# One-core Perceiver block with a routed MLP: weight folds, loads and waits in another order

## Chip, core and metric

The kernel runs on 1 core of one Trainium2 chip. The time is device microseconds of one launch. Before the change it is 768.01 us, the median of 3 runs (766.83 to 769.06).

## What is computed

16 batches of 64 tokens of width 512 pass through three residual layers. The first attends over 1601 context rows for each batch, under a mask, and ends in a layer norm with gain and bias. The second is self-attention among a batch's 64 tokens, of one head. The third sends each token to 2 of 8 experts.

```
x = x + LN(softmax(mask(norm(x) @ ctx.T / sqrt(512))) @ ctx) * gamma + beta
q, k, v = norm(x) @ W_qkv.T            # one head, 64 tokens of a batch
x = x + (softmax(q @ k.T / sqrt(512)) @ v) @ W_out.T
s = norm(x) @ router_w.T               # top 2 of 8, softmax over the two
x = x + sum_e w_e * (gelu(norm(x) @ w1[e].T) @ w2[e].T)
```

All of it is float32. There are 1024 tokens, in 8 tiles of 128 (two batches each).

## The kernel before

**Folds.** Query and key weights appear only as a product, and value and output weights too. So the kernel turns the weights on TensorE (`turn_pieces` for query and key, L757; `turn_weights` for value, L765) and multiplies them (`fold`, L773, 32 products in the profile's count): "m" goes to `scores_w`, "vo" to `values_high` and `values_low`, a high and a low part. `raw_v` and `raw_out` are the raw weights; "vo" is read by the self-attention of each tile (`values`, L879 to L881).

**Rounds.** A loop over r = 1 to 7 mixes three tiles. For tile r it computes the context scores (`scores`, L805, three blocks of 512 context rows, then `rest_scores` for the last 65). For tile r - 1 it turns probabilities (`turn_prob`, L826) and sums context rows (`sums`, L846, in the order of `PV_ORDER`: the rest, then blocks 0, 1, 2). For tile r - 2 it does self-attention: `keys` (L861), `own_scores` (L871), `values`, `turn_own_probs` (L887, the transpose of the exponentials that ScalarE made), `weigh` (L893), then turns the normed row for the router. For tile r - 3 it routes. The order on each engine is written out by hand, and PSUM banks go round in the order of `fill_order()`.

**The other engines.** VectorE does the mask and the row maximum (`softmax`), the low part of a tile (`low_xn`, L1432), the gates and places of routing (`gates`, L1472 to L1477; `route_second`, L1483 to L1488), the layer norms (`queries`, L1350 to L1358, `second_norm`, `attended`, `first_norm`), and the maximum of the own scores (`tops`, L1421, with `copy_pt`, L1428). ScalarE does exponentials and copies. GpSimd turns a tile's mask into bounds (`bounds`, L619), adds the bias (L625), and writes and reads the routing table. SyncE issues nearly all loads: the turned context (L510) and the context (L497), 1024 KB for each batch and block, each when the buffer's former reader is done; the mask (L516) when the bounds of the tile before are ready.

**End of attention and experts.** After the loop tile 7 is finished, while the first expert's weights arrive. They come as float32 and are split: ScalarE writes the high part (`split_high`), VectorE the low part (`split_low`, L1501). The rows of the first expert are gathered on GpSimd (L672), and the tokens of tiles 6 and 7, which come too late for the gather, are added by one-hot products (`hot_rows`, L930), for which VectorE first casts a list of place numbers (L1562). `keep_busy` issues transposes whose result nobody reads. Then each expert runs 16 chunks: `up`, gelu, and `down` two chunks behind (`LAG`). For the last expert VectorE scales each token tile by its gate (L1669) and GpSimd adds it to the output by an indirect DMA (L707).

## Times and profile before

| what | us |
|---|---|
| median of 3 runs | 768.01 |
| profiled execution, its own time | 767.6 |
| its span | 765.9 |
| TensorE busy in the span | 736.6 (96%) |
| VectorE busy | 443.4 (58%) |
| ScalarE busy | 309.5 (40%) |
| GpSimd busy | 153.9 (20%) |
| moved by DMA | 199.40 MB |

The page divides the span into 40 slices of 19 us. Slices 1 to 17 are context attention, the next two its end and the routing, the rest the experts. In a timeline row stand the start, the duration, engine, line, operation, output and inputs, and in brackets how long the engine was idle before and what released it. Merged rows carry a count. A float32 product appears as two instructions in the profile's count (so L846 x20 is 10 in the program). Durations of merged TensorE rows overlap the next row by 0.07 us or so.

### The profile page before, as it was taken

Reading aid. Unit: us, or ns where it says so; the run is one execution under the profiler, and the core shown is the slowest. Engines: PE = TensorE matmul, PEld = TensorE weight load, DVE = VectorE, ACT = ScalarE, POOL = GpSimd, SP = SyncE. Lnnn points to the kernel's source line nnn. Section 1 sums busy time; section 2 is a strip of 40 time slices with the busy share of each in tenths; the row PEclk is TensorE's granted clock in tenths of the full one; section 3 lists DMA queues with packets and bytes.
Section 4 is the critical chain, followed back from the end, with each engine's and each line's share of the span. In section 5 each row is a group of like instructions: output and inputs, shape, how many; then the busy total and the mean of one; then the engine's idle time right before and its main releaser. Section 6 shows DMA issues by size and latency. Waiting matters only on the chain.

```text
span 765.9 us, 12386 instructions
## 1 busy us (share of the span) xinstructions
PE 736.6 (96%) x4794; PEld 560.5 (73%) x4794; DVE 443.4 (58%) x1005; ACT 309.5 (40%) x518; POOL 153.9 (20%) x162
## 2 busy tenths in 40 slices
PE   6999999999999999999999999999999999999992
PEld 5444455454545554578999999999998998888882
DVE  5243467676767664886775545555556556555620
ACT  2022212121223221335555555565555666666620
POOL 2132130404132200132310210310211230120201
PEclk9999999999999999999999999999999999999997
DMA  9999999999999999921545545655657565665302
GB/s 328 408 419 418 398 402 418 397 419 402 418 403 417 400 416 398 330 63 32 202 165 196 143 151 194 160 193 179 185 192 199 198 227 193 214 207 216 86 1 28
DMA packets 36333, 199.40 MB, mean 260 GB/s; under 512 B 4700, under 2 KB 5100, under 8 KB 15536
## 3 DMA queue, kind: packets, MB, share of 16 engines
q1 hardware_dynamic: 29912, 186.74, 63.2%
q0 software_dynamic: 4704, 9.14, 6.4%
q10 hardware_dynamic: 1656, 2.70, 1.0%
q8 instruction: 40, 0.66, 0.3%
q14 instruction: 21, 0.17, 0.1%
HBM read 188.19 MB, written 10.37 MB: 259 GB/s over the span
## 4 chain that ended last, share of the span: by engine, by line
PE 82%; DVE 11%; issue 2%; ACT 2%; DMA 1%; POOL 0%; DVEq 0%; POOLq 0%; ACTq 0%
PE ps L805 11%; PE ps L1066 8%; PE ps L1068 8%; PE ps L1067 8%; PE ps L846 7%; PE ps L1088 4%; PE ps L1089 4%; PE ps L1090 4%; PE ps L1095 4%; PE ps L1096 4%; PE ps L1097 4%; PE ps L773 4%; DVE xn_parts L1432 2%; PE ps L826 2%; PE ps L780 1%
## 5 line engine op out<-in xcount | busy, mean ns | idle before, releaser
L479 POOL TENSOR_TENSOR small<-small 128x1 f32<-128x1 f32 x64 | 24.1, 377 | 556.3 <-DVE yb_space L1669 197.4
L1068 PE MATMUL ps<-xT,low_a 128*128 128x288 f32 (+5 forms) x384 | 110.1, 287 | 0.0
L1274 ACT ACTIVATE hid<-ps 128x288 f32<-128x288 f32 (+5 forms) x128 | 50.6, 396 | 143.7 <-PE ps L1068 141.1
L1638 DVE TENSOR_TENSOR h_ring<-hid,h_ring 128x288 fp32r<-128x288 f32 (+5 forms) x128 | 55.7, 436 | 86.1 <-ACT h_ring L1279 86.0
L1501 DVE TENSOR_TENSOR low_a<-w_raw_a,high_b 128x2048 fp32r<-128x2048 f32 x32 | 73.4, 2292 | 39.2 <-ACT high_b L1202 39.2
L846 PE MATMUL ps<-arena 128*64 128x512 f32 (+1 forms) x416 | 94.1, 597 | 0.8 <-DVE arena L1401 0.8
L805 PE MATMUL ps<-arena 128*64 128x512 f32 x384 | 85.5, 596 | 0.2 <-ACT arena L1149 0.2
L1142 ACT COPY arena<-ps 128x512 f32<-128x512 f32 (+2 forms) x89 | 41.4, 525 | 100.6 <-PE ps L780 61.3
L1066 PE MATMUL ps<-xT,high_b 128*128 128x288 f32 (+5 forms) x256 | 74.9, 292 | 0.0
L1067 PE MATMUL ps<-xT,high_b 128*128 128x288 f32 (+5 forms) x256 | 73.4, 287 | 0.0
L1068 PEld LDWEIGHTS ps<-xT,low_a 128*128 128x128 f32 x384 | 72.4, 189 | 0.0
L846 PEld LDWEIGHTS ps<-arena 128*64 128x64 f32 (+1 forms) x416 | 27.9, 136 | 54.1 <-issue 51.8
L805 PEld LDWEIGHTS ps<-arena 128*64 128x64 f32 x384 | 26.3, 137 | 48.5 <-issue 47.8
L1202 ACT CAST high_b<-w_raw_a 128x2048 fp32r<-128x2048 f32 x32 | 60.8, 1904 | 0.0
L1090 PE MATMUL ps<-h_ring,low_a 128*128 128x288 f32 (+2 forms) x192 | 56.9, 296 | 0.0
L1279 ACT CAST h_ring<-hid 128x288 fp32r<-128x288 f32 (+5 forms) x128 | 53.4, 418 | 4.1
L1066 PEld LDWEIGHTS ps<-xT,high_b 128*128 128x128 f32 x256 | 48.3, 189 | 1.4
L1067 PEld LDWEIGHTS ps<-xT,high_b 128*128 128x128 f32 x256 | 48.3, 189 | 1.1
L1501 DVE TENSOR_TENSOR low_b<-w_raw_b,high_c 128x2048 fp32r<-128x2048 f32 x16 | 36.7, 2293 | 20.6 <-ACT high_c L1202 20.5
L1501 DVE TENSOR_TENSOR low_a<-w_raw_a,high_a 128x2048 fp32r<-128x2048 f32 x16 | 36.6, 2292 | 19.9 <-ACT high_a L1202 19.9
L619 POOL TENSOR_SCALAR arena<-arena 128x1601 f32<-128x1601 int32 x8 | 45.0, 5624 | 0.0
L1377 DVE SCALAR_TENSOR_TENSOR arena<-arena,ps 128x1024 f32<-128x1024 f32 (+1 forms) x16 | 15.3, 956 | 44.8 <-PE ps L805 44.8
(217 smaller groups left out, 1644.7 us busy)
## 6 DMA issues: line engine op xcount, KB each, us to landing
arena<-in_ctx_turned SPq DMA_DIRECT2D x48, 1024.0 KB, 20.4
arena<-in_ctx SPq DMA_DIRECT2D x48, 1024.0 KB, 18.7
w_raw_a<-in_w SPq DMA_DIRECT2D x48, 1024.0 KB, 4.8
w_raw_b<-in_w SPq DMA_DIRECT2D x16, 1024.0 KB, 4.8
arena<-in_mask SPq DMA_DIRECT2D x8, 800.5 KB, 22.1
tokens_x<-arena SPq DMA_DIRECT2D x11, 256.0 KB, 12.4
arena<-in_w_qkv SPq DMA_DIRECT2D x8, 256.0 KB, 4.8
out<-res SPq DMA_DIRECT2D x8, 256.0 KB, 9.2
```

Source lines behind the costliest of these rows:

```text
L619: pool.tensor_scalar(bound, mask_sb, 0, MASKED - LIMIT, ALU.is_equal, ALU.mult).then_inc(bound_ready, 1)
L805: mm = pe.matmul(bank(blk)[64 * b:64 * b + 64, :], xqT[:, k, 64 * b:64 * b + 64], ctxT[blk][:, b, k, :], start=(k == 0), stop=(k == KC - 1))
L846: mm = pe.matmul(att_ps[64 * b:64 * b + 64, :], probT[0:m, c, 64 * b:64 * b + 64], rows, start=(n == 0 and c == chunks[0]), stop=(n == NBL ...
L1066: pe.matmul(o, w_high[2 * f][:, cols], high[:, k, 0:w.width], start=(k == 0), stop=False)
L1067: pe.matmul(o, w_high[2 * f][:, cols], low[:, k, 0:w.width], start=False, stop=False)
L1068: mm = pe.matmul(o, w_low[2 * f][:, cols], high[:, k, 0:w.width], start=False, stop=(k == KC - 1))
L1090: mm = pe.matmul(o, low[:, cols], h_high[:, 0:w.width], start=False, stop=final)
L1202: act.copy(w_high[j], w_raw[j]).then_inc(w_high_ready, 1)
L1274: nc.scalar.activation(hid[:, c % 2, 0:w.width], bank(c % UP_BANKS)[:, 0:w.width], ACT.Gelu).then_inc(gelu_done, 1)
L1279: act.copy(h_ring[:, c % RING, 0, 0:w.width], hid[:, c % 2, 0:w.width]).then_inc(h_high_ready, 1)
L1501: dve.tensor_tensor(w_low[j], w_raw[j], w_high[j].bitcast(F32), ALU.subtract).then_inc(w_ready, 1)
L1638: dve.tensor_tensor(h_ring[:, c % RING, 1, 0:w.width], hid[:, c % 2, 0:w.width], h_ring[:, c % RING, 0, 0:w.width].bitcast(F32), ALU.subtr ...
```

## The change

- Loads: value and output weights are loaded first, in eight pieces, then tile 0, then query and key weights; the constants come in two DMAs, the identity by itself first.
- Folds: value weights are turned piece by piece, and the fold "vo" comes first. Query and key weights are turned behind it, and the fold "m" comes behind tile 0's scores and the turning of tile 1's query. `bank_at`, `by_act` and the order of copies follow.
- A round: blocks 0 and 1 of `sums` move behind `turn_own_probs` and `weigh`; VectorE's `tops` moves ahead of `queries`.
- End of attention: the low part of the first expert's block 1 is made on GpSimd; `low_xn(LAST - 1)` moves ahead of `attended(LAST)`; two `keep_busy` grow or are added.
- Last expert: behind its last `up`, chunks 13, 14 and 15 of `down` are done for token tile 0 and then for token tile 1.

TensorE at the start of the program, before (L757 and L765 are transposes of weights, L773 a fold, L805 scores of tile 0, L826 the turned probabilities):

```order
L938 MATMUL ps<-cst 128x128 x16
L757 MATMUL ps<-cst,arena 128x128 x32
L773 MATMUL ps<-arena 128x512 x16
L780 MATMUL ps<-cst,arena 128x128 x4
L792 MATMUL ps<-cst,arena 128x65 x8
L805 MATMUL ps<-arena 64x512 x24
L815 MATMUL ps<-arena 64x65 x8
L765 MATMUL ps<-cst,arena 128x128 x16
L773 MATMUL ps<-arena 128x512 x16
L780 MATMUL ps<-cst,arena 128x128 x4
L792 MATMUL ps<-cst,arena 128x65 x8
L826 MATMUL ps<-cst,arena 65x128
```

and after (L760 transposes, L775 a fold, L807 scores, L828 probabilities):

```order
L940 MATMUL ps<-cst 128x128 x6
L760 MATMUL ps<-cst,arena 128x128 x16
L775 MATMUL ps<-arena 128x512 x16
L760 MATMUL ps<-cst,arena 128x128 x32
L782 MATMUL ps<-cst,arena 128x128 x4
L794 MATMUL ps<-cst,arena 128x65 x8
L807 MATMUL ps<-arena 64x512 x24
L817 MATMUL ps<-arena 64x65 x8
L782 MATMUL ps<-cst,arena 128x128 x4
L794 MATMUL ps<-cst,arena 128x65 x8
L775 MATMUL ps<-arena 128x512 x16
L828 MATMUL ps<-cst,arena 65x128
```

One fold and 16 transposes moved ahead of the scores, the other fold behind them.

VectorE in one round, before, from the queries (L1350 to L1358), which follow the places, to the tops (L1421):

```order
L1350 BN_STATS small<-res 128x6
L474 MEMSET small 128x1
L1352 BN_AGGR small<-small 128x2
L1334 TENSOR_SCALAR small<-small 128x1
L1335 TENSOR_SCALAR small<-small 128x1
L1336 SCALAR_TENSOR_TENSOR small<-small 128x1
L1338 SCALAR_TENSOR_TENSOR small<-small 128x1
L1340 SCALAR_TENSOR_TENSOR small<-small 128x1
L1342 SCALAR_TENSOR_TENSOR small<-small 128x1
L1344 SCALAR_TENSOR_TENSOR small<-small 128x1
L1358 TENSOR_SCALAR arena<-res,small 128x512
L1421 TENSOR_REDUCE small<-ps 64x1 x2
```

and after, from the places (L1488) on:

```order
L1488 TENSOR_TENSOR route<-ps,route 128x8
L1490 TENSOR_TENSOR route<-route 128x16
L1492 TENSOR_REDUCE route<-route 128x2
L1493 CAST route<-route 128x2
L1426 TENSOR_REDUCE small<-ps 64x1 x2
L1427 TENSOR_SCALAR small<-small 128x1
L473 MEMSET small 128x1
L1355 BN_STATS small<-res 128x6
```

The tops (L1426) are now the first thing behind the places, and the queries (L1355) follow.

GpSimd at the end of attention, before, from the last gathers (L672) to the sends of routing rows (L642):

```order
L672 DMA rows_space<-tokens_x,route 128x512
L479 TENSOR_TENSOR small<-small 128x1
L672 DMA rows_space<-tokens_x,route 32x512
L630 TENSOR_TENSOR small<-small 128x1
L479 TENSOR_TENSOR small<-small 128x1
L642 DMA slots_m<-route 9216x16 x2
```

and after, from the last gathers (L671) to the sends of routing rows (L641):

```order
L671 DMA rows_space<-tokens_x,route 128x512
L478 TENSOR_TENSOR small<-small 128x1
L671 DMA rows_space<-tokens_x,route 32x512
L478 TENSOR_TENSOR small<-small 128x1
L698 TENSOR_TENSOR low_a<-w_raw_a,high_a 128x2048
L629 TENSOR_TENSOR small<-small 128x1
L478 TENSOR_TENSOR small<-small 128x1
L641 DMA slots_m<-route 9216x16 x2
```

The split (L698) is new; it stands between the gather and the sends.

The diff, cut to its core:

```diff
@@ -70,16 +70,15 @@
 def fill_order():
-    for which in ("wq", "wk", "m"):
+    for which in ("wv", "vo", "wq", "wk"):
         for n in range(KC):
...
         yield kind, 0, 0
-    for which in ("wv", "vo"):
-        for n in range(KC):
-            yield which, 0, n
     for kind in ("xq", "rest0", "rest1"):
         yield kind, 1, 0
+    for n in range(KC):
+        yield "m", 0, n
     for r in range(1, TILES):
...
@@ -524,16 +523,16 @@
...
                 sp.dma_start(tokens_x[t * P:(t + 1) * P, :], xr[t % 2]).then_inc(x_out[t % 2], 16)
-            for raw, first, here in ((raw_q, 0, wq_in), (raw_k, KC, wk_in)):
+            for raw, of, first, here in ((raw_v, w_qkv, 2 * KC, wv_in), (raw_out, w_out, 0, wo_in), (raw_q, w_qkv, 0, wq_in),
+                                         (raw_k, w_qkv, KC, wk_in)):
                 for k in range(KC):
-                    sp.dma_start(raw[:, k, :], w_qkv[:, (first + k) * D:(first + k + 1) * D]).then_inc(here[k], 16)
-            sp.dma_start(res[:, 0:D], x[0:P, :]).then_inc(x_in, 16)
+                    sp.dma_start(raw[:, k, :], of[:, (first + k) * D:(first + k + 1) * D]).then_inc(here[k], 16)
+                if raw is raw_out:
+                    sp.dma_start(res[:, 0:D], x[0:P, :]).then_inc(x_in, 16)
             load_rest(0)
...
                 load_turned(0, blk)
-            sp.dma_start(raw_v, w_qkv[:, 2 * WBLK:].rearrange("p (k h) -> p k h", k=KC)).then_inc(wv_in, 16)
-            sp.dma_start(raw_out, w_out.rearrange("p (k h) -> p k h", k=KC)).then_inc(wo_in, 16)
             load_rest(1)
...
@@ -543,7 +542,7 @@
...
             load_mask(2)
-            sp.wait_ge(filled, filled_at("vo", 0, KC - 1))
+            sp.wait_ge(filled, filled_at("m", 0, KC - 1))
             load_ctx(0, 1)
...
@@ -693,6 +692,10 @@
...
             gather(STATIC[0], 3)
+            pool.wait_ge(w_high_ready, 2)
+            pool.wait_ge(w_ready, 1)
+            carry_pool_waits(pool, own)
+            pool.tensor_tensor(w_low[1], w_raw[1], w_high[1].bitcast(F32), ALU.subtract).then_inc(w_ready, 1)
             for t in range(LAST - 1, TILES):
...
@@ -759,17 +762,16 @@
...
                             mm.then_inc(filled, 1)
-            def turn_weights(kind, raw, hc):
-                o = open_fill(kind, 0, hc)
-                for k in range(KC):
-                    mm = pe.transpose(o[:, k * P:(k + 1) * P], raw[:, k, hc * P:(hc + 1) * P], ident)
-                mm.then_inc(filled, 1)
-
             def fold(kind, left, right):
...
                     for hc in range(KC):
+                        if kind == "vo" and m == 0:
+                            wait_copied(pe, "wv", 0, hc)
+                            pe.wait_ge(wo_in[hc], 16)
+                        if kind == "m" and m == 0:
+                            wait_copied(pe, "wk", 0, hc)
                         mm = pe.matmul(o, left[:, hc, m * P:(m + 1) * P], right[:, hc, :],
...
@@ -937,26 +939,23 @@
...
                     pe.transpose(o[:, 0:P], ident, ident)
-            pe.wait_ge(cst_in, 16)
-            keep_busy(16, bank(0))
+            pe.wait_ge(id_in, 16)
+            keep_busy(6, bank(0))
+            turn_pieces("wv", raw_v, wv_in)
+            fold("vo", turned_v, raw_out)
             turn_pieces("wq", raw_q, wq_in)
+            wait_copied(pe, "vo", 0, KC - 1)
             turn_pieces("wk", raw_k, wk_in)
-            for n in range(KC - 2, KC):
-                wait_copied(pe, "wk", 0, n)
-            fold("m", turned_q, turned_k)
             turn_query(0)
             turn_rest(0)
+            wait_copied(pe, "wq", 0, KC - 1)
             for blk in range(NBLK - 1):
...
             rest_scores(0)
-            pe.wait_ge(wv_in, 16)
-            for hc in range(KC):
-                turn_weights("wv", raw_v, hc)
-            pe.wait_ge(wo_in, 16)
-            wait_copied(pe, "wv", 0, KC - 1)
-            fold("vo", turned_v, raw_out)
             turn_query(1)
             turn_rest(1)
+            fold("m", turned_q, turned_k)
+            pe.wait_ge(cst_in, 16)
             for r in range(1, TILES):
...
@@ -977,14 +976,14 @@
...
                 sums(r - 1, PV_ORDER[0])
-                sums(r - 1, PV_ORDER[1])
                 if runs(r - 2):
...
                     turn_own_probs(r - 2)
-                sums(r - 1, PV_ORDER[2])
+                sums(r - 1, PV_ORDER[1])
                 if runs(r - 2):
                     weigh(r - 2)
+                sums(r - 1, PV_ORDER[2])
                 sums(r - 1, PV_ORDER[3])
...
@@ -1019,8 +1018,10 @@
...
             router(LAST)
-            keep_busy(18, open_fill("rank", LAST))
+            keep_busy(23, open_fill("rank", LAST))
             ranks(LAST)
+            wait_copied(pe, "logit", LAST)
+            keep_busy(5, bank(bank_at("logit", LAST)))
             hot_rows(LAST)
...
@@ -1091,20 +1092,27 @@
...
                     for t, (a, m) in enumerate(w.tiles):
+                        if only is not None and t != only:
+                            continue
                         o = bank(y_bank(w, t))[0:m, :]
...
                             mm.then_inc(first_tile_done, 1)
-                mm.then_inc(down_done, 1)
+                if only != 0:
+                    mm.then_inc(down_done, 1)
             for w in STATIC:
...
                     up(w, c)
-                    if c >= LAG:
+                    if w.kind == EXPERTS - 1 and c == FC - 1:
+                        for t in range(2):
+                            for late in range(FC - 1 - LAG, FC):
+                                down(w, late, t)
+                    elif c >= LAG:
                         down(w, c - LAG)
...
@@ -1117,9 +1125,6 @@
...
                     more = in_use(pe)
-            for c in range(FC - LAG, FC):
-                down(STATIC[-1], c)
-
             with pe.If(more > 0):
...
@@ -1201,28 +1206,28 @@
...
                 act.copy(w_high[j], w_raw[j]).then_inc(w_high_ready, 1)
-            act.dma_start(cst[:], consts).then_inc(cst_in, 16)
-            act.wait_ge(cst_in, 16)
-            act.copy(small[:, 26:27], me)
-            for kind, dst in (("wq", turned_q), ("wk", turned_k)):
-                for n in range(0, KC, 2):
-                    copy_fill(kind, 0, dst[:, n, :], n)
+            act.dma_start(ident, consts[:, C_ID:C_ID + P]).then_inc(id_in, 16)
+            act.wait_ge(id_in, 16)
+            act.copy(small[:, 26:27], ident[:, 0:1])
+            for n in range(0, KC, 2):
+                copy_fill("wv", 0, turned_v[:, n, :], n)
+            act.dma_start(cst[:, C_TRI:], consts[:, C_TRI:]).then_inc(cst_in, 16)
             act.dma_start(res[:, D:2 * D], x[P:2 * P, :]).then_inc(x1_in, 16)
...
             act.dma_start(rw_sb, w_router.rearrange("p (k e) -> p k e", k=KC)).then_inc(rw_in, 16)
-            for n in range(0, KC, 2):
-                copy_fill("m", 0, scores_w[:, n, :], n)
-            copy_query(0)
-            copy_rest(0)
-            for n in range(KC):
-                copy_fill("wv", 0, turned_v[:, n, :], n)
-            exps(0)
             for n in range(KC):
...
                 act.copy(values_high[:, n, :], bank(bank_at("vo", 0, n))).then_inc(vo_high, 1)
-            copy_query(1)
-            copy_rest(1)
+            for kind, dst in (("wq", turned_q), ("wk", turned_k)):
+                for n in range(0, KC, 2):
+                    copy_fill(kind, 0, dst[:, n, :], n)
+            for p in range(2):
+                copy_query(p)
+                copy_rest(p)
+            exps(0)
+            for n in range(0, KC, 2):
+                copy_fill("m", 0, scores_w[:, n, :], n)
             act.wait_ge(zero_out, 16)
...
@@ -1509,23 +1514,25 @@
...
             own.then_next(dve.memset(cum[0], 0.0))
+            for n in range(1, KC, 2):
+                copy_fill("wv", n, turned_v[:, n, :])
+            queries(0)
             dve.wait_ge(cst_in, 16)
...
                 own.then_next(dve.memset(capacity[:, p:p + 1], float(WIDTHS[p])))
-            for kind, dst in (("wq", turned_q), ("wk", turned_k)):
-                for n in range(1, KC, 2):
-                    copy_fill(kind, n, dst[:, n, :])
-            queries(0)
-            for n in range(1, KC, 2):
-                copy_fill("m", n, scores_w[:, n, :])
-            softmax(0)
-            queries(1)
             for n in range(KC):
...
                                   ).then_inc(copied[False], 1)
+            for kind, dst in (("wq", turned_q), ("wk", turned_k)):
+                for n in range(1, KC, 2):
+                    copy_fill(kind, n, dst[:, n, :])
+            queries(1)
+            softmax(0)
+            for n in range(1, KC, 2):
+                copy_fill("m", n, scores_w[:, n, :])
             for r in range(1, TILES):
...
@@ -1535,22 +1542,22 @@
...
                     route_second(r - 3)
+                if runs(r - 2):
+                    tops(r - 2)
                 if runs(r + 1):
...
                 if runs(r - 2):
-                    tops(r - 2)
                     copy_pt(r - 2)
...
             route_first(LAST - 2)
-            for j in range(2):
-                split_low(STATIC[0], j)
+            split_low(STATIC[0], 0)
             gates(LAST - 2)
             route_second(LAST - 2)
+            low_xn(LAST - 1)
             attended(LAST)
-            low_xn(LAST - 1)
             tops(LAST - 1)
...
@@ -1567,6 +1574,7 @@
...
             second_norm(LAST)
+            dve.wait_ge(w_ready, 2)
             split_low(STATIC[0], 2)
```

## Rows read from the trace of the kernel before

**Rows 1.** The page's slices: busy DMA in tenths, and GB/s.
```profile
DMA  9999999999999999921545545655657565665302
GB/s 328 408 419 418 398 402 418 397 419 402 418 403 417 400 416 398 330 63 32 202 165 196 143 151 194 160 193 179 185 192 199 198 227 193 214 207 216 86 1 28
```

**Rows 2.** Timeline of TensorE, tile 0's scores and the fold behind them.
```profile
29.41 10.52 PE L805 MATMUL ps<-arena 128*64 128x512 f32 x48 [0.19 <-ACT arena L1149]
...
43.17 13.97 PE L773 MATMUL ps<-arena 128*128 128x512 f32 x32 [0.88 <-issue]
```

**Rows 3.** SyncE's loads: tile 0's last turned blocks (L510), tile 4's mask (L516).
```profile
L510 SPq DMA_DIRECT2D arena<-in_ctx_turned x2: 522/523/524, 8.8 to 9.4; - x2
...
DMA to landing us min/median/max: 20.3/21.6/22.8
...
L516 SPq DMA_DIRECT2D arena<-in_mask x1: 327/327/327, 107.2 to 107.2; - x1
...
DMA to landing us min/median/max: 27.8/27.8/27.8
```

**Rows 4.** Timeline of TensorE in rounds 3 (146.78) and 4.
```profile
146.78 0.33 PE L887 MATMUL ps<-cst,own_space 128*128 128x128 f32 x1 [1.48 <-ACT own_space L1183]
...
175.18 4.51 PE L846 MATMUL ps<-arena 65*64 65x512 f32 x20
...
183.24 0.33 PE L887 MATMUL ps<-cst,own_space 128*128 128x128 f32 x1
```

**Rows 5.** Timeline of GpSimd and VectorE in rounds 3 and 4.
```profile
135.28 5.61 POOL L619 TENSOR_SCALAR arena<-arena 128x1601 f32<-128x1601 int32 x1
...
142.32 0.69 DVE L1350 BATCH_NORM_STATS2 small<-res 128x6 f32<-128x512 f32 x1
...
178.78 0.69 DVE L1350 BATCH_NORM_STATS2 small<-res 128x6 f32<-128x512 f32 x1
...
181.68 0.47 DVE L1421 TENSOR_REDUCE small<-ps 64x1 f32<-64x64 f32 x2
```

**Rows 6.** Two lines of VectorE over the span: ns least/median/most.
```profile
L1432 DVE TENSOR_TENSOR xn_parts<-arena,xn_parts x8: 682/1810/4309, 99.5 to 332.7; 128x512 fp32r<-128x512 f32 x8
...
L1472 DVE CAST route<-route x8: 158/606/1052, 139.9 to 351.8; 128x2 int32<-128x2 f32 x8
```

**Rows 7.** TensorE's waits: us in total, times, longest.
```profile
PE ps L879 <- DVE xn_parts L1432: 0.7, 1, 0.7
```

**Rows 8.** Timeline of VectorE at the end of attention.
```profile
312.34 4.49 DVE L1501 TENSOR_TENSOR low_a<-w_raw_a,high_a 128x2048 fp32r<-128x2048 f32 x2 [1.05 <-ACT high_a L1202]
...
333.29 0.30 DVE L1562 CAST arena<-arena 128x288 f32<-128x288 int32 x1
...
334.47 0.48 DVE L1421 TENSOR_REDUCE small<-ps 64x1 f32<-64x64 f32 x2 [0.87 <-PE ps L871]
...
338.45 0.29 DVE L1428 COPY own_space<-ps 128x128 f32<-128x128 f32 x1 [0.32 <-PE ps L887]
```

**Rows 9.** Timeline of GpSimd: the bias of one tile, the last gather.
```profile
255.10 1.28 POOL L625 TENSOR_TENSOR res<-res,arena 128x512 f32<-128x512 f32 x1
...
332.97 1.17 POOL L672 DMA_INDIRECT rows_space<-tokens_x,route  x1
```

**Rows 10.** Hot rows of tiles 6 and 7; one microsecond with its granted clock (0.50).
```profile
342.77 2.21 PE L930 MATMUL ps<-arena 128*128 128x288 f32 x8
...
351.25 3.66 PE L930 MATMUL ps<-arena 128*128 128x288 f32 x8 [0.66 <-DVE arena L1496]
...
352.00:353.00 1.00, 1.00 (x4) 0.70 (x3) 0.90 (x5) 0.40 (x1) 0.19 (x1) 0.50 0.00 0
```

**Rows 11.** Chain of waits at the end: start, us, what.
```profile
751.33 0.24 PE ps L1097
...
751.60 0.76 DVE yb_space L1669
...
755.19 1.48 POOL out L707
```

12 lines of the change are left out of this document (6 added, 6 removed).

## Prediction

> **What bounds the kernel now.** I read the engine totals first: TensorE is busy 96% of the span, so time can only come from its waits, from work done at a low clock, and from the two ends. The list of waits names few: the start, a transpose that waits for a ScalarE exponential (L887), products that wait for the low part of a tile (L879) [rows 7]. The page's slices of DMA show a second resource at its limit: about 410 GB/s without a pause until some 325 us, that is, through the whole attention stage [rows 1]. TensorE never waits for DMA there, but it is not far ahead of it. So every microsecond saved at the front has to be checked against landings, and every order inside a round against VectorE. All times below are from one profiled execution of 767.6 us (span 765.9), 0.4 under the median of the runs, 768.0. I work out a difference and add it to the median.
>
> **Part 1, the opening.** Value and output weights (8 pieces of 256 KB, 2.1 MB) now go ahead of query, key and tile 0's context; the fold of value and output comes first and the fold of query and key behind tile 0's scores. TensorE's work is the same but for 10 fewer filler transposes. What changes is the landing of tile 0's turned context. Its last block was issued at 9.4 us and landed 22.8 later, at 32.2 [rows 3], and scores began at 29.41 with three blocks in 10.52 us, so the third block was read at 36.4 [rows 2], 4 us behind its landing. With 2.1 MB more ahead of it in the queue, at 0.41 MB/us [rows 1], it lands at 37.3. However early TensorE gets to the scores, they end at 37.3 + 3.5 = 40.8 rather than 39.9. The gain comes behind them: before, 3.2 us lay between the end of the scores (39.93) and the start of the second fold (43.17) [rows 2], mostly transposes of the value weights and a short wait; these now lie ahead of the scores, where the landing hides them. With the scores 0.9 later, I put the front at some 2 us earlier from round 1 on (3.2 less 0.9, a little more or less for the copies behind the fold).
>
> The waits that the opening adds hold nothing up that I can find. Key's transposes wait until VectorE has split the last value fold, while query's 16 transposes run. SyncE's wait ahead of context blocks 1 and 2 is now for the fold of query and key, which ends where the other one ended. VectorE's wait for the constants, now a separate DMA, stands behind the first queries and ahead of the value splits; TensorE needs those only for the keys, some 10 us on. If the constants landed that late, the loss would still lie under the wait for the context.
>
> I count none of it. Round 3 is tied to something that does not move: the mask for tile 4. It was issued at 107.2, when the bounds of tile 3 were ready, and landed 27.8 us later, at 135.0 [rows 3], behind a queue whose bytes are the same after the change. At 135.28 GpSimd starts on it for 5.61 us, until 140.9 [rows 5]. VectorE's operations that need the port which GpSimd then holds stand still: L1432, at best 682 ns, took 4309 in this round, and the small cast L1472, 158 ns at best, 1052 [rows 6]. The chain to tile 1's exponentials goes through that cast, so TensorE's L887 of round 3 has a floor in absolute time.
>
> **Part 2, the order inside a round.** TensorE's sums of the first large block go behind own scores, values and the transpose L887; VectorE looks for the own tops (L1421) ahead of the next tile's queries. Two things follow. The tops can start where the queries started: 142.32 in round 3, 178.78 in round 4 [rows 5]. From tops to the transpose it takes 183.24 - 181.68 = 1.56 us [rows 4, 5]. But one block of sums, 16 of the 20 instructions that took 4.51 us, 3.6 us [rows 4], now comes after the transpose rather than before it.
> - Round 3: L887 at 142.32 + 1.56 = 143.88, and with the block behind it 147.48, where the round before was at 146.78 (it had waited 1.48) [rows 4]. That is 0.70 later, whatever the opening had gained.
> - Round 4: 178.78 + 1.56 + 3.6 = 183.94 against 183.24: 0.70 more. TensorE itself would be ready for the transpose by about 183.24 - 3.6 = 179.6, against 180.34 from VectorE: a new wait of 0.7. Rounds 5 and 6 repeat round 4's rows (three of this kind in all), so 0.70 each.
> - Round 2 has no gating work for VectorE and round 7 no bounds on GpSimd; I count 0 there. In round 2 the transposed probabilities (L1428) now stand behind queries that GpSimd blocks, up to a microsecond, but round 3 swallows that.
> Sum for the rounds: 4 x 0.70 = 2.8 us later. The bounds are 0 (if VectorE is released sooner) and, with the front's gain kept as well, -2; on the other side +5, should L1428, which now stands behind the queries (2.9 us from 178.78 to 181.68), hold `weigh` up by half a microsecond more in each.
>
> **Part 3, the end of attention.** One of VectorE's two splits of expert weights (4.49 us for two, 2.25 each [rows 8]) goes to GpSimd, and the low part of tile 6 is ahead of the long `attended(LAST)`. The wait of 0.7 us at L879 goes [rows 7], and I shift VectorE's work behind it by 0.7. But GpSimd's split has a place and a price. GpSimd does it behind the gather, whose last part started at 332.97 and took 1.17 [rows 9]. The gather hangs on the routing that stood behind the two splits, so it ends 2.25 earlier, at 331.9, and the split starts near 332.1. A GpSimd tensor_tensor of 128x512 takes 1.28 us [rows 9]; four times that is 5.1. Below it is VectorE's 2.25 for the same tensor, above nothing nearer. In this time, from 332.1 to 337.4, VectorE wants the cast of place numbers (L1562), at 333.29 - 0.7 = 332.6 [rows 8]. It has the short form of L1472's kind (288 columns in 0.30 us), so I take it to be blocked as L1472 was. Tops of tile 7 then start near 337.7 rather than at 334.47: 3.2 later. Of that 0.32 comes back where VectorE had waited at L1428 [rows 8]. Cost 2.9 us, since from there VectorE and TensorE alternate until the experts begin. The bounds are -0.7 (no blocking) and +5.1 (all of it in the way). VectorE's new wait for that split, ahead of its third one, is met long before; so are GpSimd's sends behind it, whose gates come after VectorE's routing.
>
> The Trainium skill (GPSIMD Engine Reference, section on elementwise cost) gives 4.5 us on GpSimd for a tensor_tensor of 2048 float32 columns against 2.29 on VectorE. The second agrees with the trace here; by the first the cost of this part would be 2.3 rather than 2.9.
> The trace shows the blocking only beside L619, a GpSimd operation of one input. The Trainium skill (SBUF — State Buffer, "Who interferes with whom") states that it holds against any GpSimd operation that reads SBUF, for VectorE operations of two SBUF inputs or in a two-port mode, and that the one that issues first keeps the port. By it the routing operations behind the cast would be held back even if the cast got through, and the cost would be about 1 us.
>
> **Part 4, filler and clock.** Before, the hot rows of tile 7 took 3.66 us where the same eight instructions for tile 6 took 2.21, with the granted clock at 0.50 in that stretch, the 1.2 GHz level, after some 2 us in which TensorE did little [rows 10]. Five more filler transposes ahead of the ranks and five behind them close that gap and fit into the waits that they fill. Gain 1.45, if the clock holds; 0 if not; a loss of 1.2 if all ten delay the ranks (128 columns each where one of the eight, 0.28 us, had 288: 0.12).
>
> **Part 5, the last expert.** Behind the last `up`, TensorE did three chunks for both token tiles, tile 0's last product being followed by tile 1's. VectorE scaled tile 0 at 751.60 and GpSimd sent out the second part at 755.19, two sends in a row [rows 11]. Now all of tile 0 comes first: its result is ready 6 products earlier, of 0.24 us each [rows 11], 1.4 us, less some 0.2 for the last hidden chunk, which now has less cover. GpSimd's sends are serial, so both go out 1.2 earlier; tile 1's own result comes at most 0.2 later and finds the queue free. Gain 1.2, at least 0.5, at most 1.4.
>
> **Sum.** +2.8 + 2.9 - 1.45 - 1.2 = +3.05. On the profiled execution this is 770.6, on the median 771.1. I forecast 770.8.
>
> **Rivals.**
> - A, the forecast: the rounds get a wait, GpSimd's split holds VectorE up, filler and end pay. 770.8, own range 769 to 772.5. For it: VectorE is the last releaser at L887 in both rounds that I read, and a port conflict is in the trace. Against it: starts of GpSimd's work are rough.
> - B, the split on GpSimd is free: it starts later than I think or doesn't hold the port. Part 3 is then -0.7 and the sum +2.8 - 0.7 - 1.45 - 1.2 = -0.55: 767.4, no change. This is the case that isn't slower. It decides at L1562: if the cast starts under 333.3, less what the rounds added, B holds. For it: the cast and GpSimd's start are within 0.5 us of each other in my working.
> - C, round 3 isn't pinned, VectorE finishes its routing before GpSimd takes the port, and the front's 2 us stay while rounds 4 to 6 lose nothing: -2 - 0.7 - 1.45 - 1.2 = -5.4: 762.6; with part 3's cost, 766.2. It needs VectorE to be more than 2.2 us earlier in round 3 than before; DMA allows about 1 there.
> - D, the clock falls as well: in A TensorE has, by my working, little to do for some 4 us ahead of the row products, longer than the 2 us that preceded the fall at 352. The row products (about 5 us) would then run at 1.65 times their length as the hot rows did, up to 3.3 more: 774.
>
> **Chances.** A 0.42, B 0.25, C 0.17, D 0.16. A measurement of this kernel can tell 0.3%, 2.3 us, from no change: faster is under 765.7, slower over 770.3. A gives 0.27 slower and 0.15 the same; D 0.16 slower; B 0.20 the same and 0.05 faster; C 0.04 the same and 0.13 faster. So faster 0.18, same 0.39, slower 0.43. The range 764.5 to 774 leaves out the better half of C and the far end of D.
>
> **What would show it.** In the changed profile: the third block of tile 0's scores waits for a landing near 37 us; L887's successor waits for ScalarE 3 us in round 3 and 0.7 in rounds 4 to 6, and the starts of rounds 4 to 7 stand 0.7, 1.4, 2.1 and 2.8 later than before; a VectorE cast of 128x288 takes 4 to 5 us beside GpSimd's split; the last hot rows take 2.2 us at a granted clock of 1.0; VectorE's two last scalings stand apart in start, by more than the 0.7 of one, rather than in one piece. The forecast is wrong if rounds 3 to 6 show no new wait at the transpose (C), or the cast takes 0.3 us (B).

## The result, and the profile after

The changed kernel takes 778.57 us (median, 775.22 to 780.16), the kernel before 767.42 in the same comparison: ratio 1.0137, 95% interval 1.0099 to 1.0176. It is slower by 1.4%, where 0.4% was forecast. The profiled execution took 778.62 us with a span of 777.0, so 11.1 more than the span of before. The page's slices, to be held against [rows 1]:

```profile
PEclk9999999999999999979999999999999999999997
DMA  8999999999999998910445644745665756574402
GB/s 299 385 417 418 395 402 417 400 419 401 419 401 417 398 416 353 338 60 29 147 163 179 171 148 167 212 127 216 170 226 173 211 185 229 188 244 171 126 1 27
```

Two things are new. The first two slices moved 299 and 385 GB/s, and one slice, from 330 to 350 us, has a granted clock of 0.7. The opening, on TensorE (start, duration, idle before and what ended it), to be held against [rows 2]:

```profile
29.28 3.65 PE L807 MATMUL ps<-arena 128*64 128x512 f32 x16 [0.27 <-ACT arena L1154]
35.73 3.65 PE L807 MATMUL ps<-arena 128*64 128x512 f32 x16 [2.80 <-DMA arena<-in_ctx_turned]
41.34 3.65 PE L807 MATMUL ps<-arena 128*64 128x512 f32 x16 [1.95 <-DMA arena<-in_ctx_turned]
46.38 1.93 PE L775 MATMUL ps<-arena 128*128 128x512 f32 x4
```

TensorE was ready for tile 0's scores when it was before, waited twice for landings, and read the third block at 41.3 rather than at the forecast 37.3. Windows of before and of after show most of the reason (length, busy time of each engine, granted clock, DMA share, GB/s):

```profile
5.00:10.00 5.00, 5.00 (x24) 5.00 (x25) 0.80 (x10) 0.13 (x1) 0.00 (x0) 1.00 1.04 373
10.00:20.00 10.00, 8.79 (x40) 5.47 (x39) 8.04 (x16) 2.74 (x5) 5.39 (x2) 1.00 1.03 387
20.00:30.00 10.00, 9.81 (x36) 4.79 (x36) 2.10 (x3) 1.73 (x4) 1.84 (x3) 1.00 1.03 415
```
```profile
5.00:10.00 5.00, 4.92 (x23) 4.55 (x22) 0.81 (x2) 1.07 (x2) 0.00 (x0) 1.00 0.92 289
10.00:20.00 10.00, 10.00 (x24) 4.30 (x24) 5.20 (x25) 1.17 (x2) 0.00 (x0) 1.00 1.06 359
20.00:30.00 10.00, 9.29 (x58) 6.41 (x58) 5.16 (x13) 4.46 (x9) 5.77 (x2) 1.00 1.02 392
```

From 5 to 30 us before moved 5 x 0.373 + 10 x 0.387 + 10 x 0.415 = 9.9 MB, after 9.0. The missing 0.9 MB are 2.3 us of the queue at 0.41 MB/us.

TensorE's waits from 121 to 300 us (us in total, times, longest), first of before, then of after:

```profile
PE ps L887 <- ACT own_space L1183: 1.6, 2, 1.5
```
```profile
PE ps L889 <- ACT own_space L1188: 3.3, 4, 1.5
```

The transpose of own probabilities waits 1.49 us in round 3 (1.48 before, [rows 4]) and 0.62, 0.60 and 0.60 in rounds 4 to 6. The wait of [rows 7], for the low part of a tile, is gone. Rounds 3 to 7 begin 2.97, 2.97, 3.47, 3.93 and 4.43 us later than before. The end of attention is where most is lost. VectorE, GpSimd and TensorE there:

```profile
336.58 4.64 DVE L1341 SCALAR_TENSOR_TENSOR small<-small 128x1 f32<-128x1 f32 x1
336.65 4.54 POOL L698 TENSOR_TENSOR low_a<-w_raw_a,high_a 128x2048 fp32r<-128x2048 f32 x1
342.10 0.55 DVE L1363 TENSOR_SCALAR arena<-res,small 128x512 f32<-128x512 f32 x1
342.70 1.11 PE L782 MATMUL ps<-cst,arena 128*128 128x128 f32 x4 [4.51 <-DVE arena L1363]
```

GpSimd's split took 4.54 us. A VectorE operation on one column, 0.22 us when nothing is in its way, took 4.64 beside it and ended at 341.22, 0.03 us behind the split. It belongs to tile 6's normalization, for which TensorE then waited 4.51 us. Behind that wait TensorE's clock was low (windows of TensorE: busy time, granted clock, DMA share, GB/s):

```profile
338.00:342.00 4.00, 0.19 (x2) 0.93 0.00 0
342.00:346.00 4.00, 3.30 (x26) 0.50 0.35 131
346.00:350.00 4.00, 4.00 (x12) 0.50 0.00 0
352.00:356.00 4.00, 3.73 (x28) 1.00 0.00 0
```

0.50 is the 1.2 GHz level. The products of tile 7's values started 0.43 us apart there, those of tile 6's values 0.23 us apart. The last hot rows, for their part, now ran at the full clock, to be held against [rows 10], and the two outputs of the last expert stood apart, to be held against [rows 11]:

```profile
364.93 2.21 PE L932 MATMUL ps<-arena 128*128 128x288 f32 x8
```
```profile
762.66 0.75 DVE L1677 TENSOR_SCALAR yb_space<-ps,route 128x512 f32<-128x512 f32 x1 [1.06 <-PE ps L1100]
764.75 0.75 DVE L1677 TENSOR_SCALAR yb_space<-ps,route 112x512 f32<-112x512 f32 x1 [1.34 <-PE ps L1100]
```

The 11.1 us between the two profiled executions divide as follows. Opening and rounds make 4.4 until round 7 begins. The sums of tile 7 behind the loop make 1.5; the granted clock fell to 0.50 there, between 310 and 315 us. From there to the transpose of tile 7's own probabilities it is 7.8 (351.77 against 338.08, 13.7 in all). Then the filler gains 1.5 and the last expert 1.1.

### The profile page after: what moved, and what is told of

Read it like the earlier page. It is cut to its first block, busy times and chain, and to the rows that moved or that the text cites. A ratio compares the mean times of both kernels' runs of the same rounds, so it can differ in the third digit from the quotient of the medians.

```text
span 777.0 us, 12399 instructions
## 1 busy us (share of the span) xinstructions
PE 741.4 (95%) x4794; PEld 562.3 (72%) x4794; DVE 440.4 (57%) x1006; ACT 308.6 (40%) x516; POOL 159.2 (20%) x164
## 4 chain that ended last, share of the span: by engine, by line
PE 79%; DVE 7%; DMA 6%; SPq 3%; issue 1%; ACT 1%; POOL 0%; DVEq 0%; POOLq 0%; ACTq 0%
PE ps L848 10%; PE ps L807 9%; PE ps L1067 8%; PE ps L1069 8%; PE ps L1068 8%; PE ps L1089 4%; PE ps L1090 4%; PE ps L1091 4%; PE ps L1098 4%; PE ps L1099 4%; PE ps L1100 4%; DMA arena<-in_ctx_turned 3%; DMA arena<-in_ctx 3%; PE ps L775 2%; PE ps L782 1%
## 5 line engine op out<-in xcount | busy, mean ns | idle before, releaser
L848 PE MATMUL ps<-arena 128*64 128x512 f32 (+1 forms) x416 | 96.0, 606 | 1.3 <-DVE arena L1406 0.9
L807 PE MATMUL ps<-arena 128*64 128x512 f32 x384 | 85.9, 596 | 5.4 <-DMA arena<-in_ctx_turned 5.2
L807 PEld LDWEIGHTS ps<-arena 128*64 128x64 f32 x384 | 26.4, 137 | 54.2 <-issue 46.4
L1506 DVE TENSOR_TENSOR low_a<-w_raw_a,high_a 128x2048 fp32r<-128x2048 f32 x15 | 34.4, 2292 | 19.9 <-ACT high_a L1207 19.9
```

Source lines behind the costliest of these rows:

```text
L807: mm = pe.matmul(bank(blk)[64 * b:64 * b + 64, :], xqT[:, k, 64 * b:64 * b + 64], ctxT[blk][:, b, k, :], start=(k == 0), stop=(k == KC - 1))
L848: mm = pe.matmul(att_ps[64 * b:64 * b + 64, :], probT[0:m, c, 64 * b:64 * b + 64], rows, start=(n == 0 and c == chunks[0]), stop=(n == NBL ...
L1506: dve.tensor_tensor(w_low[j], w_raw[j], w_high[j].bitcast(F32), ALU.subtract).then_inc(w_ready, 1)
```

## The experiments

Each was timed against the kernel before on the same chip. Ratios are to the kernel before, with 95% intervals. The experiments fall into three such comparisons, in which the kernel before took 767.69 us (1, 2, 4 and 6), 767.98 (3, 8, 9 and 10) and 768.22 (5, 7, 11 and 12). A gain or loss is counted from the one of its own comparison; between kernels of two comparisons, or against the changed kernel, some 0.5 us are uncertain from this alone.

**1. The change without GpSimd's split** (a_no_gpsimd_split).

```diff
...
-            pool.tensor_tensor(w_low[1], w_raw[1], w_high[1].bitcast(F32), ALU.subtract).then_inc(w_ready, 1)
...
-            split_low(STATIC[0], 0)
+            for j in range(2):
+                split_low(STATIC[0], j)
...
-            dve.wait_ge(w_ready, 2)
```

> The changed kernel, with one edit taken back: VectorE makes both low halves of expert weights behind round 7 (blocks 0 and 1), as before the change; GpSimd none. Theory S (GpSimd's 4.54 us split held VectorE's normalization of tile 6 for 4.64 us, and the low clock from 342 to 351 us followed from TensorE's 4.5 us wait): both go, at the price of 2.25 us of VectorE: about 4.5 + 3.8 - 0.5 = 7 to 9 us less than the changed kernel's 778.6, so 770 to 771. The transpose of attended rows that waited 4.51 waits under 2, and values of tile 7 run at 0.23 us per product. Rival R (the low clock at 342 is not the wait's doing, but comes by itself, as that at 309 to 316 did): only the 4 to 5 us of blocking go, 774, and a stretch at a granted clock of 0.50 remains between 335 and 360. Rival F (the split is free, the loss lies in the front and the rounds): within 1 us of 778.6.

Measured: 770.13 us (768.37 to 772.49), ratio 1.0031 (1.0012 to 1.0051). This one edit is worth 8.4 of the 11 us by the medians (8.1 by the ratios); the changed kernel has only four runs. TensorE in the same windows as above:

```profile
338.00:342.00 4.00, 4.00 (x27) 1.00 0.28 106
342.00:346.00 4.00, 3.77 (x28) 1.00 0.00 0
346.00:350.00 4.00, 3.71 (x23) 1.00 0.30 96
```

Both the wait and the low clock are gone, as theory S has it.

**2. The split alone** (b_split_only): on the kernel before, the reverse of the edit above.

> The kernel before, with one edit: the low half of expert weight block 1 is made by GpSimd behind its gather for tile 7, and VectorE makes one half fewer there. Theory S: GpSimd holds VectorE for 4 to 4.6 us at an operation that stands at about 326 to 332 us, TensorE waits 4 us or more behind it and the clock falls to 0.50 afterwards: +5 to +9, so 773 to 776. Theory A of the forecast (the cast of 288 columns is held, no fall of the clock): +2.9, 770.9. Rival F (free): -0.7 to 0, 767.3.

Measured: 772.28 us, ratio 1.0055 (1.0023 to 1.0087), and the widest spread of all: 767.49 to 778.37 in 12 runs. Four runs took 776.9 to 778.4 us at a mean granted clock of 0.982 to 0.984, three some 772.5 at 0.986, and five 767.5 to 771.1 at 0.990 to 0.993. So the long runs fit theory S and the shortest fit rival F. Only one run has a trace, 777.46 us, one of the long ones:

```profile
332.49 5.09 DVE L1342 SCALAR_TENSOR_TENSOR small<-small 128x1 f32<-128x1 f32 x1
```
```profile
333.04 4.51 POOL L699 TENSOR_TENSOR low_a<-w_raw_a,high_a 128x2048 fp32r<-128x2048 f32 x1
```

What is held is the small operation behind the one of the changed kernel, in the same normalization. Its row ends with the split (337.58 and 337.55) but starts 0.55 us ahead of it, while the last gather ran. The split's 4.5 us are fixed. That VectorE stands still for all of them or not at all, by what it has to do as the split starts, is how I read the spread; no short run of this kernel has a trace that would show it.

**3. Filler in TensorE's wait** (a_filler_wait).

```diff
+            keep_busy(36, open_fill("xr", LAST - 1))
             turn_second(LAST - 1)
```

> The changed kernel, with 36 more filler transposes (some 0.12 us each, 4.3 us) ahead of the transposes of tile 6's normalized rows, where TensorE waits 4.5 us for VectorE, which GpSimd's split holds. The split stays on GpSimd. Theory S (the fall to a granted clock of 0.50 from 342 to 351 us follows from TensorE's wait): the clock stays at 1.00, values of tile 7 take 0.23 us per product, and the time is 3 to 4 less than 778.6, 774.6 to 775.6; the wait for VectorE stays. Rival R (the fall has another cause, the long attention stage): a stretch of 0.50 of some 9 us remains and the time is 778.6.

Measured: 775.09 us (771.98 to 776.68), ratio 1.009 (1.0072 to 1.0107), 3.5 under the changed kernel. The mean granted clock of its six runs is 0.987 to 0.995, that of the changed kernel's four 0.983 to 0.990. Time and clock are those of theory S, but the profile doesn't prove it: in the profiled run, the fastest of the six, GpSimd's split started behind all of tile 6's normalization and held nothing that TensorE waited for.

```profile
336.99 0.37 DVE L1570 CAST arena<-arena 128x288 f32<-128x288 int32 x1
```
```profile
337.40 4.54 POOL L698 TENSOR_TENSOR low_a<-w_raw_a,high_a 128x2048 fp32r<-128x2048 f32 x1
```

There the filler itself was in the way (TensorE was in it from 336.27 to 340.2) and the clock stayed at 1.00. That the clock falls behind a wait and stays up without one is seen in five traces at the end of attention: it fell to 0.50 in experiments 2 and 4 and in the changed kernel, behind waits of 4.5 us and more, and in experiment 5 behind one of 1.86, and did not fall in experiment 1. That filler alone holds it up through a held normalization stays open.

**4. Query and key weights in one transfer each** (a_qk_whole).

```diff
+                if raw is raw_q or raw is raw_k:
+                    sp.dma_start(raw, of[:, first * D:(first + KC) * D].rearrange("p (k h) -> p k h", k=KC)).then_inc(here[0], 16)
+                    continue
```

> The changed kernel, with query weights and key weights each loaded by one transfer of 1 MB, whose rows are 8 KB, in place of four of 256 KB with rows of 2 KB. Theory L (small rows lower the rate of the first 20 us, 268 to 390 GB/s where the kernel before had 373 to 420): the rate from 6 to 24 us rises to about 400, the third block of tile 0's turned context lands at 38 to 39 rather than 41.3, and the time falls by 1 to 2.5 us, 776 to 777.5. Rival H (the rate is that of the hardware's start, whatever the rows): landing unchanged within 0.5 us; the transposes of the query weights start later, as their four pieces come together, and the time is the same or up to 2 us more.

Measured: 777.55 us (776.32 to 778.48), ratio 1.0115 (1.0084 to 1.0146). The third block of tile 0 was read at 38.91 instead of 41.34, and scores of tile 1 began at 59.38 instead of 61.82, 2.4 us sooner, so theory L is right for the landing. Of that 1.5 us were gone again when round 3 began, at 123.55 against 124.45. The time is 1 us under the changed kernel's, which is within both intervals. Two of the waits of its round 2:

```profile
88.97 3.65 PE L810 MATMUL ps<-arena 128*64 128x512 f32 x16 [0.86 <-DMA arena<-in_ctx_turned]
94.07 3.65 PE L810 MATMUL ps<-arena 128*64 128x512 f32 x16 [0.86 <-DMA arena<-in_ctx_turned]
```

TensorE had caught up with the transfers there. What the opening gains beyond them is lost again. GpSimd's split held VectorE in this kernel too: the same operation as in the changed kernel took 4.95 us and ended with the split, at 340.65.

```profile
335.70 4.95 DVE L1344 SCALAR_TENSOR_TENSOR small<-small 128x1 f32<-128x1 f32 x1
```
```profile
336.10 4.52 POOL L701 TENSOR_TENSOR low_a<-w_raw_a,high_a 128x2048 fp32r<-128x2048 f32 x1
```

**5. GpSimd's split behind tile 6's normalization** (a_split_late).

```diff
             pool.wait_ge(w_ready, 1)
+            pool.wait_ge(xn_split, TILES)
```

> The changed kernel, with one more wait: GpSimd begins its split only when VectorE has written the low part of tile 7, that is behind tile 6's normalization. Theory S (the 4.6 us hold falls on whatever VectorE issues as the split starts; what matters is that it was the normalization, for which TensorE waits): VectorE's normalization takes its 0.22 us, TensorE's wait there falls from 4.5 to about 1 us, the clock stays at 1.00: 769.5 to 772. Rival T (VectorE's later operations of two inputs, tops and routing of tile 6, are held in turn until the split ends): the hold moves, 773 to 776, and the spread over runs gets smaller than that of the changed kernel.

Measured: 773.58 us (772.5 to 774.38), ratio 1.0072 (1.005 to 1.0093), and the narrowest spread of the kernels with a split (1.9 us; experiment 4, whose split isn't tied, has 2.2). Rival T is right. GpSimd's split, and VectorE beside it:

```profile
339.52 4.58 POOL L699 TENSOR_TENSOR low_a<-w_raw_a,high_a 128x2048 fp32r<-128x2048 f32 x1
```
```profile
339.06 0.30 DVE L1570 CAST arena<-arena 128x288 f32<-128x288 int32 x1
340.49 0.48 DVE L1427 TENSOR_REDUCE small<-ps 64x1 f32<-64x64 f32 x2 [1.12 <-PE ps L874]
341.00 0.15 DVE L1428 TENSOR_SCALAR small<-small 128x1 f32<-128x1 f32 x1
341.60 0.16 DVE L1459 TENSOR_REDUCE route<-route 128x1 f32<-128x8 f32 x1
341.79 2.33 DVE L1462 SCALAR_TENSOR_TENSOR route<-route,cst 128x8 f32<-128x8 f32 x1
344.16 0.16 DVE L1464 TENSOR_REDUCE route<-route 128x1 f32<-128x8 f32 x1
```

Reductions and a one-column operation on one input and constants go through at their usual length. The first operation with two inputs from SBUF stands until the split ends at 344.10. TensorE then waited 1.86 us for routing, and the clock was at 0.50 from 348 to 350. This kernel is 5.4 us over the kernel before and experiment 1 is 2.4 over it, so the split, moved out of the worst place, still costs 3 us.

**6. The new opening alone** (b_front_only): weight loads, folds and copies as in the change, all else as before.

> The kernel before, with the new opening alone: value and output weights in 8 pieces ahead of query and key, their fold first, the fold of query and key behind tile 0's scores, identity and constants as two transfers. Order inside the rounds, filler, last expert and splits as before. Theory L (landings set the opening: 5 us of the queue's early rate is lost to the 8 more transfers of 2 KB rows): third block of tile 0's context lands at 41, scores of tile 1 1 to 1.5 us later, and the rounds, tied to the masks' landings, +1.5 to +3: 769.5 to 771. Forecast's own step: 0 (the front gains 2, round 3 takes it back): 768. Rival G (the fronts' loss is absorbed by the wait of 1.48 us at round 3's transpose): within 0.5 us of before.

Measured: 769.38 us (767.05 to 772.97), ratio 1.0022 (1.0003 to 1.0042), 1.7 slower. The third block of tile 0 was read at 40.46, scores of tile 1 began 0.6 later than before and round 3 2.0 later. The wait in round 3 shrank from 1.48 to 0.52, so that rounds 4 to 7 began 1.07 later. Theory L and rival G share it: the landings come later, and the wait absorbs a part.

**7. The new opening with the output weights in one transfer** (b_front_out_whole): on experiment 6, one load of 1 MB for `raw_out`, and one wait for it.

> The kernel before with the new opening alone, and the output weights loaded by one transfer of 1 MB in place of four of 256 KB. Theory L1 (the dip to 170 to 270 GB/s between 5 and 8 us comes from the output weights' small rows): it goes, 10 us of queue deliver 2.8 MB as in the kernel before, not 2.3, third block of tile 0's context lands some 1 us sooner. Rival L2 (the dip has to do with the transfers of value weights and constants, or with two tensors at once): it stays, and the time is that of the opening alone, 769.4.

Measured: 767.59 us (765.09 to 769.76), ratio 1.0001 (0.9982 to 1.002). The dip between 5 and 10 us is mostly gone:

```profile
5.00:10.00 5.00, 3.92 (x21) 3.49 (x19) 1.19 (x2) 1.07 (x2) 0.00 (x0) 1.00 0.97 350
```

Scores of tile 1 began at 59.31, 1.6 sooner than in experiment 6. In the profiled runs with the old opening they began between 59.49 and 60.65 (six traces), in those with the new one and its loads in pieces between 60.94 and 62.81 (five), and with some of these loads whole between 59.18 and 59.38 (experiments 4, 7 and 12). So theory L1 holds for the landing, though TensorE itself came to tile 0's scores later here, at 31.96 rather than 29.34. The two intervals of the ratio overlap (1.0003 to 1.0042 in experiment 6), so a gain in time isn't shown.

**8. The order in the rounds alone** (b_rounds_only).

```diff
                 sums(r - 1, PV_ORDER[0])
-                sums(r - 1, PV_ORDER[1])
...
                     turn_own_probs(r - 2)
-                sums(r - 1, PV_ORDER[2])
+                sums(r - 1, PV_ORDER[1])
                 if runs(r - 2):
                     weigh(r - 2)
+                sums(r - 1, PV_ORDER[2])
                 sums(r - 1, PV_ORDER[3])
```

together with the edit of experiment 9.

> The kernel before, with the new order in the rounds alone: the second large block of sums goes behind own scores, values and the transpose of own probabilities, and VectorE looks for the own tops ahead of the next tile's queries. Theory W (each of rounds 4 to 6 waits 0.6 us at that transpose and takes 36.97 us instead of 36.5; round 3 waits 1.5, as before): +1.4 to +2.8, 769.1 to 770.5. Rival N (those waits come from the opening's delay, and with the old opening the rounds are free): within 0.5 of before.

Measured: 770.2 us (767.39 to 773.3), ratio 1.0026 (1.0012 to 1.004), 2.2 slower. Its waits are those of the changed kernel: 1.48 in round 3, 0.62, 0.62 and 0.61 in rounds 4 to 6, each of these rounds 36.97 us long against 36.46 to 36.52 before. Theory W holds. The transpose of round 4:

```profile
180.30 0.33 PE L887 MATMUL ps<-cst,own_space 128*128 128x128 f32 x1 [0.62 <-ACT own_space L1183]
```

**9. Tops ahead of the next queries, alone** (b_tops_only).

```diff
+                if runs(r - 2):
+                    tops(r - 2)
                 if runs(r + 1):
                     queries(r + 1)
                 if runs(r - 2):
-                    tops(r - 2)
                     copy_pt(r - 2)
```

> The kernel before, with one edit: VectorE looks for the own tops (some 1.5 us) ahead of the next tile's queries. The sums' order stays. Theory W: own probabilities are ready sooner by the queries' length, the waits at the transpose (1.48 in round 3, 0.16 in round 5) go, while the queries and what hangs on them have cover: -0.5 to -1.6, 766.1 to 767.2. Rival M (round 3 is tied to the mask's landing and GpSimd's bounds, the tops cannot start before): 0, 767.7.

Measured: 765.57 us (762.65 to 766.45), ratio 0.9963 (0.9946 to 0.9981), 2.4 faster, more than theory W allowed. No wait at the transpose is left, and rounds 3 to 6 take 36.13 us each. That goes for round 3 too, although GpSimd's bounds start at 136.19 in it, so rival M is refuted. The transpose of round 4, then VectorE in that round, first of experiment 9, then of experiment 8:

```profile
181.13 0.27 PE L887 MATMUL ps<-cst,own_space 128*128 128x128 f32 x1
```

```profile
178.69 0.48 DVE L1421 TENSOR_REDUCE small<-ps 64x1 f32<-64x64 f32 x2 [1.41 <-PE ps L871]
```
```profile
178.74 0.47 DVE L1421 TENSOR_REDUCE small<-ps 64x1 f32<-64x64 f32 x2
```

Counted from the round's start on TensorE (157.47 and 159.29), VectorE was ready for the tops after 19.8 us in experiment 9 (it then waited 1.41 for its input) and after 19.5 in experiment 8. Its chain is as long in both. But TensorE comes to the transpose after 23.7 us in experiment 9 and after 20.4 in experiment 8, where the probabilities are there after 21.0.

**10. Filler, last expert and the low part of tile 6, alone** (b_ends_only): the changed kernel's three edits of that kind on the kernel before.

> The kernel before, with the end of attention's filler (23 transposes ahead of the last ranks, 5 behind), the low part of tile 6 ahead of the attended rows of tile 7, and the last expert's order (all of token tile 0 first). No split on GpSimd, old opening and rounds. By the changed kernel's trace: filler -1.5 (hot rows 2.21 us at the full clock, not 3.66), last expert -1.1, low part -0.7 to 0: 764.5 to 765.2. Rival P (filler only moves the low clock elsewhere, or the last send is bound by the queue): 766.5 to 767.7.

Measured: 765.16 us (763.32 to 769.24), ratio 0.9962 (0.9948 to 0.9976), 2.8 faster, as the trace of the changed kernel had it. (Its profiled run, 769.24 us, is the slowest of the ten.)

**11. What gained, together** (c_tops_ends): experiments 9 and 10 on the kernel before.

> The kernel before, with the parts that gained when each was made alone: VectorE's tops ahead of the next queries (2.4 us less), and filler, last expert's order and early low part of tile 6 (2.8 us less). They lie in different stages, so they should add: 767.8 - 5.2 = 762.6. Rival Q (both gains partly hide one another, as with a wait for the masks or the clock's chance): 764 to 765.

Measured: 762.95 us (761.91 to 763.9), ratio 0.9938 (0.9917 to 0.9959). The two gains add: 2.4 + 2.8 = 5.2 expected, 5.3 measured. This kernel is faster than the changed kernel and than the kernel before.

**12. The same with the new opening, its loads whole** (c_tops_ends_front): only the value weights still come in four pieces.

> The same, with the new opening too, where output, query and key weights are loaded by one transfer of 1 MB each and only the value weights in four pieces. Theory L (the opening loses because the queue delivers 0.9 MB less in the first 30 us; with whole transfers most of that comes back): within 1 us of the kernel without the new opening, 762 to 763.5. Rival K (the new opening costs its 1.7 us through something else, such as the later issue of context blocks 1 and 2): 764.3 or more. Rival J (scores of tile 1 begin 1 us sooner than in the kernel before, and with the tops early nothing in round 3 takes it back): 761.5.

Measured: 762.57 us (761.87 to 764.02), ratio 0.9935 (0.9915 to 0.9956). With whole transfers the opening costs nothing, and gains nothing that these runs can tell. Scores of tile 1 began at 59.18 here and 60.65 in experiment 11, round 3 at 121.89 and 121.43, the transpose of round 7 came at 290.09 and 289.82. The 1.5 us are lost by round 3.

## Why the prediction was wrong, point by point

**Sign and size.** Slower was right and the likeliest case, but the time lay 4.6 us above the range. The largest error is in part 3: GpSimd's split, put at 2.9 us, cost 8.4.

**Part 1, the opening: the DMA term was mis-sized.** The forecast took 0.41 MB/us from the queue with 2.1 MB more in it. The third block was read as it landed, at 41.3, not 37.3. In the first 30 us the queue delivered 0.9 MB less than before, which makes 2.3 of these 4.0 us. And 14.3 MB had moved when the block landed (346 GB/s over 41.3 us) against 11.7 before (363 over 32.2), so 2.6 MB more rather than 2.1, which makes another 1.2; the rest is a rate of 363 GB/s from 35 to 40 us. The rate fell to 166 GB/s between 6 and 7 us in experiment 6, while the output weights' four transfers of 256 KB were under way, and was 334 in the same microsecond with one of 1 MB. The gain of 2 us that I put behind the scores became 1.5 us later at tile 1's scores. The claim that round 3 would take any such difference was half right: alone the opening costs 1.7 us, not 0.

**The pin of round 3 was not a fixed time.** I had put its floor at tile 4's mask landing at 135.0 and GpSimd's bounds [rows 3, 5]. In the changed kernel that mask was issued at 112.1 rather than at 107.2 and landed at 138.6, and round 3 began 2.97 us later with the same wait of 1.49 behind it. In experiment 6 the round began 2.0 later and its transpose stood 1.07 later. So the floor moves, by a part or all of the round's own delay. And it isn't the mask's: in experiment 9 the bounds hold VectorE in round 3 as well (an operation of 0.16 us on it took 3.46), and with the tops ahead of the queries nothing waits.

**Part 2, the order in a round: right in place, close in size.** Forecast: a wait of 3 us in round 3 and 0.7 in rounds 4 to 6, starts of rounds 4 to 7 later by 0.7 each. Measured: waits of 1.49 and 0.6; 0.5 more in each of rounds 4 to 6 and nothing in round 3. In experiment 8, without the opening, it makes 2.2 us where 2.8 were forecast. By the rows, 1.5 us of that stand until round 7, all of them in rounds 4 to 6; that the two sums are so near is in part luck. The wait of 3 us was not even what my own rows gave: TensorE ready at 141.7 and the transpose at 143.88 make 2.2. What the forecast did not see is that the part has two halves of opposite sign: tops early gain 2.4 us (experiment 9), so the order of the sums on top of them costs the difference of the two experiments, 4.6. That order was not timed without the early tops. I had priced both together against rounds of 36.5 us and never asked what a round takes without waits, 36.13.

**Part 3, GpSimd's split: the step that failed.** I put the split at 332.1, the cast of place numbers beside it, and the cost at 2.9. The split started at 336.65, 4.5 us later than I had it, while TensorE was 6.0 later than before there (its last sums ended at 323.66 against 317.70); so GpSimd was some 1.4 us earlier against VectorE's work, and it met tile 6's normalization. The cast came at 343.16, behind the split, and took 0.30 us. That was my sign for B, yet the split was far from free. The mechanism of rival A was right (a held VectorE operation), the victim was wrong, and the bound of +5.1 for "all of it in the way" was too low since it left out the clock: rival D gave that 3.3 us behind other work. Held operation and clock together make 8.4 us (experiment 1). I had priced D as A plus a fall of the clock at 774, with a chance of 0.16, and both came together on top of the opening's loss. B, the free split, is possible: in the profiled run of experiment 3 the split held nothing, and the shortest run of experiment 2 (767.49) has the time for it, but no trace.

The Trainium skill (GPSIMD Engine Reference, section on elementwise cost) gives 4.5 us for such an operation; my estimate from the 128x512 row was 5.1, the trace has 4.54. Of the shared port, the Trainium skill (SBUF — State Buffer, "Who interferes with whom") says that a GpSimd operation that reads SBUF holds back VectorE operations of two SBUF inputs or in a two-port mode. Experiment 5 agrees: the operation of two inputs was held for 2.33 us, reductions were not; the one-column operations held in the changed kernel and in experiment 2 have two inputs as well. I had put the cost of held routing at about 1 us by that rule; experiment 5, where routing is what is held, has it at 3 us, a fall of the clock included.

**Part 4, filler: right.** The forecast was -1.45; the last hot rows went from 3.66 to 2.21 us at a granted clock of 1.00.

**Part 5, last expert: right.** The forecast was -1.2. At the first `up` (355.98 before, 368.21 after) the changed kernel was 12.2 us behind and at the end 11.1, so it gained 1.1. Experiment 10 has parts 4 and 5 and the low part at 2.8.

**The sum, by experiments.** Opening +1.7, rounds +2.2, ends -2.8 make +1.1; experiment 1 has them together at +2.4. The difference of 1.3 is no more than the intervals leave room for. A part of it can be seen in the traces: alone the opening shrinks round 3's wait by 1 us, with the new order it doesn't. The split adds 8.4, against 4.6 alone. The spreads suggest that more runs meet the hold in the changed kernel (four runs, the lowest 775.22) than in experiment 2; why the two engines meet there more often was not tested.

## What to carry to other kernels

Work moved to GpSimd to relieve VectorE is priced by what VectorE has to do while it runs, not by the saved time: here 2.25 us saved cost 8.4, and 4.6 on the kernel before. Look for a stretch in which VectorE has mainly reductions and reads of PSUM. A single input is not safe by itself: a cast of 0.17 us took 0.98 beside the bounds in round 3. Where the start of GpSimd's split was not tied to the normalization beside it, one kernel's runs differed by up to 11 us (experiment 2); tied, they differed by 1.9 (experiment 5). With six runs, and 2.2 in experiment 4 without a tie, that is a hint and no proof. Reorderings come in bundles: time each half alone, since a loss of 4.6 hid a gain of 2.4 here. And where a stage runs at the rate of the transfers, an earlier start gains only as far as bytes are ahead.

## What the runs showed of the hardware

- A GpSimd operation of 4.51 to 4.58 us held a VectorE operation on a single column for 4.64 us (changed kernel), 5.09 (experiment 2) and 4.95 (experiment 4), and one on eight columns for 2.33 (experiment 5). In all four the held operation's row ends 0.02 to 0.03 us behind GpSimd's. In the first three it starts 0.07 to 0.55 us ahead of GpSimd's row. GpSimd's rows are rough, so which of the two was first is not shown. That an operation is narrow is no protection.
- Four transfers of 256 KB of one tensor, behind four of another, moved 286 GB/s from 5 to 10 us, and one of 1 MB in their place 350. The kernel before had 373 with eight small ones of one tensor, so the size of a transfer is not the whole cause; the rest stays open.
- Between 304 and 316 us the granted clock fell to 0.50 for 3 to 4 us in the profiled runs of the changed kernel and of experiments 2, 4, 6, 7, 8 and 10, and not in those of 1, 3, 5, 9, 11 and 12 nor before. The sums there took 6.21 us instead of 4.51, behind the same wait of 0.8 to 0.9 us in either case. What decides was not tested. The changed kernel and those of experiments 3 and 5 are alike up to this place, and the clock fell in the first alone, so 1.7 us of the differences between traces are of this kind.
